# A graph layer on one core: gathers that add to the edge product in place of copy and addition

## The reference

```python
h = concatenate([x[src], edge_attr], axis=1)       # 53125 x (128 + 64)
h = relu(_bn(h @ W1 + b1, g1, be1))                # mean and variance over all edges
s = segment_sum(h, dst); cnt = segment_sum(1, dst)
agg = s / max(cnt, 1)
h2 = relu(_bn(concatenate([x, agg], axis=1) @ W2 + b2, g2, be2))
out = layernorm(x + relu(h2 @ Wl + bl))
```

## Time and profile before

| what | value |
|---|---|
| median of 3 runs | 901.51 us (897.14 to 904.6) |
| profiled execution: span | 892.4 us, 11876 instructions |
| median less that span | 9.1 us |
| POOL / PE / DVE / ACT busy | 461.4 / 455.6 / 389.9 / 235.3 us |
| gathers (L597) | 416, from 52.6 to 725.0 us |
| stretch after them | 167.4 us of the span |

### The profile page before, as it was taken

How to read it: one execution, slowest core, us unless ns; L and a number is a source line. 1 busy time by engine, 2 the same in 40 slices (tenths; PEclk the granted TensorE clock), 3 DMA queues, 4 the chain that set the end, 5 groups by cost and what they waited for, 6 DMA issues and landing times.

```text
span 892.4 us, 11876 instructions
## 1 busy us (share of the span) xinstructions
PE 455.6 (51%) x2195; PEld 345.1 (39%) x2195; DVE 389.9 (44%) x905; ACT 235.3 (26%) x595; POOL 461.4 (52%) x572
## 2 busy tenths in 40 slices
PE   1644454535525455334544543354543349999662
PEld 1622232323323233223332332232332239998542
DVE  1343434334333343333434433244433267776495
ACT  0111122212212122111322222121221135655264
POOL 2046666566665655556666655565655543333352
PEclk9955555555555555555555555555555558999887
DMA  1233322223323222223332322232322224777202
GB/s 64 86 89 88 92 87 80 88 79 94 100 85 88 76 88 88 69 84 94 92 94 76 96 77 77 82 98 72 94 85 71 85 89 131 210 223 226 90 1 72
DMA packets 65229, 83.87 MB, mean 94 GB/s; under 512 B 19159, under 2 KB 44168, under 8 KB 65217
## 3 DMA queue, kind: packets, MB, share of 16 engines
q1 hardware_dynamic: 40529, 39.49, 15.2%
q0 software_dynamic: 13312, 27.29, 11.2%
q10 hardware_dynamic: 11376, 16.97, 5.2%
HBM read 63.61 MB, written 20.08 MB: 94 GB/s over the span
## 4 chain that ended last, share of the span: by engine, by line
another core or an unknown queue 30%; PE 26%; issue 16%; DMA 7%; ACT 6%; DVE 5%; POOL 3%; SPq 2%; ACTq 2%; DVEq 2%; POOLq 1%
PE psH L715 12%; PE psT L709 3%; DMA res<-spill 3%; PE psH L770 3%; PE psC L770 3%; POOL work L597 3%; ACT work L846 2%; ACT res L863 2%; DMA res<-in_x 2%; SPq L404 2%; PE psH L695 1%; PE psC L725 1%; ACTq L857 1%; DMA work<-ytab,idx 1%
## 5 line engine op out<-in xcount | busy, mean ns | idle before, releaser
L597 POOL DMA_INDIRECT work<-ytab,idx x416 | 398.7, 958 | 320.5 <-DVE idx L992 143.3
L715 PE MATMUL psH<-w1e,work 128*128 128x256 f32 x416 | 214.7, 671 | 350.0 <-ACT work L846 254.4
L715 PEld LDWEIGHTS psH<-w1e,work 128*128 128x128 f32 x416 | 121.6, 322 | 409.8 <-ACT work L846 278.1
L1052 DVE TENSOR_TENSOR work<-psH,work 128x512 f32<-128x512 f32 x104 | 71.9, 691 | 235.8 <-remote 104.7
L846 ACT ACTIVATE work<-psT 128x256 f32<-128x256 f32 x104 | 39.9, 384 | 474.2 <-remote 326.2
L1066 DVE TENSOR_TENSOR psX<-work,psX 128x512 f32<-128x512 f32 x104 | 72.1, 693 | 116.7 <-ACT work L861 76.2
L1152 DVE TENSOR_TENSOR work<-res,psX 128x512 f32<-128x512 f32 x103 | 70.7, 688 | 26.5 <-PE psC L770 12.4
L861 ACT ACTIVATE work<-work 128x512 f32<-128x512 f32 x104 | 65.3, 627 | 60.3 <-issue 33.2
L1059 DVE TENSOR_TENSOR psS<-work,psS 128x512 f32<-128x512 f32 x104 | 71.7, 689 | 2.4 <-issue 2.4
L709 PE MATMUL psT<-ident,work 128*128 128x128 f32 x208 | 68.0, 430 | 8.5 <-DMA work<-in_edge_attr 7.7
L617 POOL TENSOR_TENSOR agg<-agg,srci 128x64 f32 x104 | 32.3, 310 | 66.2 <-ACT srci L910 64.5
(11 more groups left out here) (144 smaller groups left out, 336.0 us busy)
## 6 DMA issues: line engine op xcount, KB each, us to landing
work<-in_edge_attr SPq DMA_DIRECT2D x103, 128.0 KB
work<-ytab,idx POOLq DMA_INDIRECT x416
hot_dram<-hotb ACTq DMA_DIRECT2D x26, 256.0 KB
spill<-work ACTq DMA_DIRECT2D x26, 256.0 KB
res<-spill SPq DMA_DIRECT2D x25, 256.0 KB, 2.9
hotb<-hot_dram SPq DMA_DIRECT2D x13, 256.0 KB, 3.9
work<-hot_dram SPq DMA_DIRECT2D x13, 256.0 KB, 3.2
h2x_dram<-agg ACTq DMA_DIRECT2D x25, 125.0 KB
```

Of the source, the lines that this page charges most:

```text
L597: pool.indirect_dma_start(yg[:, q % 2, j * F:(j + 1) * F], None, ytab, bass.IndirectOffsetOnAxis(ap=idx[:, q, j:j + 1], axis=0)).then_inc( ...
L715: last = pe.matmul(psH[q % 2][:, b * 2 * F:(b + 1) * 2 * F], eat[:, q % 2, b * P:(b + 1) * P], w1e[:, :, :].rearrange("p a f -> p (a f)"), ...
L1052: dve.tensor_tensor(hs[:, q % 2, :], psH[q % 2][:, :], yg[:, q % 2, :], ALU.add).then_inc(h_ready, 1)
```

## The change

The rows of the table are no longer gathered into a buffer of their own. ACT first copies the edge product from PSUM to the group's final place, `res` or, for the fourth group of a body, one tile `away` (`part`); then the gather adds the rows of the table to it (`compute_op=ALU.add`). DVE's addition `make_h` and the buffers `yg` and `hs` are gone, as is ACT's copy to `res`; squares and sum read the final place. The gathers take their indices directly from `srci`, so `stage_idx` and `idx` are gone; for this the 104 groups are written out on POOL, without a loop. There are four `gathered` semaphores, one for each group of a body, instead of two.

The order changes as well. PE's step `q` is now the product of `q+2`, the transposes of `q+3`, the counts of `q`. ACT's is the squares of `q`, `part` of `q+2`, `turned` of `q+3`. The hardware loops of PE and ACT have one body less, the last but one being written out too. On POOL a gather waits for `part` of its group and for the sum of the group four back.

```diff
 @block.gpsimd
+            pool.wait_ge(s_idx, 1)
+
             def gather(i, q):
-                if not first(i, q, 2):
-                    pool.wait_ge(h_ready, U * i + q - 1)
-                pool.wait_ge(idx_staged, U * i + q + 1)
-                pool.sem_inc(slot_passed, 1)
+                g = U * i + q
+                if g >= U:
+                    pool.wait_ge(h_summed, g - U + 1)
+                pool.wait_ge(z_ready, g + 1)
+                rows = res[:, (i * KEEP + q) * GF:(i * KEEP + q + 1) * GF] if q < KEEP else away
                 for j in range(TILES):
                     pool.indirect_dma_start(
-                        yg[:, q % 2, j * F:(j + 1) * F], None, ytab,
-                        bass.IndirectOffsetOnAxis(ap=idx[:, q, j:j + 1], axis=0)
-                    ).then_inc(gathered[q % 2], 16)
-
-            for q in range(U):
-                gather(0, q)
-            with pool.Fori(1, NI) as i:
+                        rows[:, j * F:(j + 1) * F], None, ytab,
+                        bass.IndirectOffsetOnAxis(ap=srci[:, j, g:g + 1], axis=0), compute_op=ALU.add
+                    ).then_inc(gathered[q], 16)
+
+            for i in range(NI):
                 for q in range(U):
                     gather(i, q)
 @block.tensor
             def edge_step(i):
+                turned_out = not (isinstance(i, int) and i == NI - 1)
                 for q in range(U):
-                    product(i, q)
-                    if q == 0 and not (isinstance(i, int) and i == 0):
-                        pe.wait_ge(x_out, i)
+                    if q + 2 < U:
+                        product(i, q + 2)
+                    elif turned_out:
+                        product(i + 1, q + 2 - U)
+                    if q + 3 < U:
+                        turn(i, q + 3)
+                    elif turned_out:
+                        turn(i + 1, q + 3 - U)
+                    if q == 2 and turned_out:
+                        pe.wait_ge(x_out, i + 1)
                     counts(i, q)
-                if not (isinstance(i, int) and i == NI - 1):
-                    x_product(i)
+                    if q == 1 and turned_out:
+                        x_product(i)
 @block.scalar
-            def store(i, q):
-                act.wait_ge(h_ready, g + 1)
+            def part(i, q):
+                g = U * i + q
+                act.wait_ge(prod_ready, g + 1)
+                if q == KEEP and not (isinstance(i, int) and i == 0):
+                    act.wait_ge(spilled, 16 * i)
+                    act.wait_ge(sq_ready, g - U + 1)
+                    act.wait_ge(h_summed, g - U + 1)
+                if isinstance(i, int) and i == NI - 1 and q == 0:
+                    act.wait_ge(x_ps, NT)
+                act.sem_inc(slot_passed, 1)
+                act.activation(slot(i, q), psH[q % 2][:, :], ACT.Copy).then_inc(z_ready, 1)
+
+            def squares(i, q):
+                g = U * i + q
+                act.wait_ge(gathered[q], 64 * (i + 1))
...
-                act.activation(sq[:, q % 2, :], hs[:, q % 2, :], ACT.Square).then_inc(sq_ready, 1)
-                if q < KEEP:
-                    act.activation(resg(i, q), hs[:, q % 2, :], ACT.Copy).then_inc(kept, 1)
+                act.sem_inc(slot_passed, 1)
+                act.activation(sq[:, q % 2, :], slot(i, q), ACT.Square).then_inc(sq_ready, 1)
             def edge_step(i):
+                over = isinstance(i, int) and i == NI - 1
                 for q in range(U):
...
+                    squares(i, q)
+                    if q + 2 < U:
+                        part(i, q + 2)
+                    elif not over:
+                        part(i + 1, q + 2 - U)
+                    if q + 3 < U:
+                        turned(i, q + 3)
+                    elif not over:
+                        turned(i + 1, q + 3 - U)
+                    if q == 1 and not (isinstance(i, int) and i == NI - 1):
+                        x_product_out(i)
 @block.vector
             def edge_step(i):
                 for q in range(U):
-                    make_h(i, q)
-                    if not (isinstance(i, int) and i == NI - 1):
-                        stage_idx(i + 1, q)
                     if q < U - 1:
                         onehot_b(i, q + 1)
                     elif not (isinstance(i, int) and i == NI - 1):
                         onehot_b(i + 1, 0)
+                    add_counts(i, q)
                     sum_h(i, q)
-                    add_counts(i, q)
```

More of the change, by code:

```diff
@@ L93, in gnn_kernel @@
         work = sb("work", [P, 6, GF])
-        yg = work[:, 0:2, :]
-        hs = work[:, 2:4, :]
+        away = work[:, 0, :]
         sq = work[:, 4:6, :]
@@ L107, in gnn_kernel @@
         srci = sb("srci", [P, TILES, NG], I32)
-        idx = sb("idx", [P, U, TILES], I32)
         loc = sb("loc", [P, TILES, NG])
@@ L225, in gnn_kernel @@
         prod_ready = sem("ea_product_ready")
-        idx_staged = sem("idx_staged")
-        gathered = [sem(f"gathered{i}") for i in range(2)]
-        h_ready = sem("h_ready")
+        gathered = [sem(f"gathered{i}") for i in range(U)]
+        z_ready = sem("z_ready_in_slot")
         sq_ready = sem("sq_ready")
@@ L232, in gnn_kernel @@
         s_folded = sem("sums_folded")
-        kept = sem("kept")
         spilled = sem("spilled")
@@ L302, in resg, with slot @@
             return res[:, bass.ds((i * KEEP + q) * GF, GF)]
+        def slot(i, q):
+            return resg(i, q) if q < KEEP else away
         def sq_fold(k):
@@ L700, in _, with turn @@
             pe.wait_ge(s_wsgn, 2)
-            def product(i, q):
+            def turn(i, q):
                 g = U * i + q
@@ L710, in product @@
                 last.then_inc(ea_turned, 1)
+            def product(i, q):
+                g = U * i + q
                 pe.wait_ge(eat_ready, g + 1)
                 if not first(i, q, 2):
-                    pe.wait_ge(h_ready, g - 1)
+                    pe.wait_ge(z_ready, g - 1)
                 for b in range(2):
@@ L729, in x_product @@
             def x_product(i):
-                pe.wait_ge(cnt_added, U * i + U - 1)
+                pe.wait_ge(cnt_added, U * i + 1)
                 for h in range(H2):
@@ L737, in edge_step @@
             def edge_step(i):
+                turned_out = not (isinstance(i, int) and i == NI - 1)
                 for q in range(U):
-                    product(i, q)
-                    if q == 0 and not (isinstance(i, int) and i == 0):
-                        pe.wait_ge(x_out, i)
-                    counts(i, q)
-                if not (isinstance(i, int) and i == NI - 1):
-                    x_product(i)
+                    if q + 2 < U:
[8 more added lines that the diff above has]
+                        pe.wait_ge(x_out, i + 1)
+                    counts(i, q)
+                    if q == 1 and turned_out:
+                        x_product(i)
+            turn(0, 0)
+            turn(0, 1)
+            product(0, 0)
+            turn(0, 2)
+            product(0, 1)
             edge_step(0)
-            with pe.Fori(1, NI - 1) as i:
+            with pe.Fori(1, NI - 2) as i:
                 edge_step(i)
+            edge_step(NI - 2)
             edge_step(NI - 1)
@@ L846, in turned @@
                 act.activation(eat[:, q % 2, :], psT[q % 2][:, 0:2 * P], ACT.Copy).then_inc(eat_ready, 1)
-            def store(i, q):
+            def part(i, q):
                 g = U * i + q
-                act.wait_ge(h_ready, g + 1)
+                act.wait_ge(prod_ready, g + 1)
[10 more added lines that the diff above has]
+                act.wait_ge(gathered[q], 64 * (i + 1))
                 if q == KEEP:
-                    act.dma_start(spill[bass.ds(i, 1), :, :].rearrange("a p f -> (a p) f"), hs[:, q % 2, :]
-                                  ).then_inc(spilled, 16)
+                    act.dma_start(spill[bass.ds(i, 1), :, :].rearrange("a p f -> (a p) f"), away).then_inc(spilled, 16)
                 elif q == KEEP - 1:
@@ L874, in edge_step @@
             def edge_step(i):
+                over = isinstance(i, int) and i == NI - 1
                 for q in range(U):
[L876 to L880, removed]
-                if not (isinstance(i, int) and i == NI - 1):
-                    x_product_out(i)
+                    squares(i, q)
[9 more added lines that the diff above has]
+                        x_product_out(i)
             act.wait_ge(s_idx, 1)
             turned(0, 0)
+            turned(0, 1)
+            part(0, 0)
+            turned(0, 2)
+            part(0, 1)
             edge_step(0)
             act.wait_ge(s_tab, TAB)
-            with act.Fori(1, NI - 1) as i:
+            with act.Fori(1, NI - 2) as i:
                 edge_step(i)
+            edge_step(NI - 2)
             edge_step(NI - 1)
@@ L1010, in _ @@
             link(dve.tensor_copy(srci[:, :, :].rearrange("p j g -> p (j g)"), psS[:, 0:TILES * NG]))
-            for q in range(U):
```

(8 more changed lines are left out.)

2 lines of the change are left out of this document (removed).

## The result

The changed kernel takes 997.82 us (median of 4 runs, 996.13 to 998.16) against 901.45 us of the kernel before beside it (4 runs, 897.14 to 904.6): slower, ratio 1.1074, 95% interval 1.1025 to 1.1122. Where the executions of a kernel fall into a quicker and a slower group, ratios and intervals here compare the quicker ones alone. The profiled execution has a span of 996.4 us; 892.4 before.

What follows compares the result with a forecast made beforehand. It took POOL's gather pitch, 1.26 us, as the floor: last gather at 580.5 instead of 724.97, with the end -145.2, giving 756, plus 37 for PE's late answers: 793 us, range 748 to 938.

Steps and rivals of the forecast that it cites:

- the lower end: POOL's gathers: adding in flight costs nothing, so a gather stays at 0.958 us.
- The upper end: POOL's gathers: three row ends instead of two make a gather 1.44 us, +0.48.
- The second rival: POOL's 416 gathers become dear: with +0.48 us each, pitch 1.74, 956 us in all; chance 0.26.
- 157.6 us of waits: POOL's waits before gathers, 143.3 us for staged indices and 14.3 for DVE's addition: what a better edge loop can return.
- PE's late answers: PE's results come late while POOL issues gathers: ten pieces of 13.5 to 13.8 us, taken as a property that may stay.
- The 37 us: Edge loop: the part of PE's late answers not covered by working two groups ahead, added to 756 us.
- the first rival: Edge loop, clean POOL bound: the new order dissolves PE's late answers, so the 37 us go too, 756 us; chance 0.20.
- ten of them last 13.7, so 3.6 stick out of each: Edge loop: two groups ahead cover 10.1 us of each late answer of PE, leaving 36 us.
- The third rival: Before gathers, POOL waits for the product instead of the index, same 157.6 us: about 904 us; chance 0.08.

Runs made afterwards that it cites:

- e1_plain: The changed kernel with gathers that overwrite instead of adding: 754.65 us, beside 753.75 for the kernel before; ratio 1.001.
- e2_add_alone: The kernel before with only its gathers made to add into their buffer: 990.82 us, where the kernel before takes 753.75.
- The half gathers: The changed kernel with gathers over 64 partitions instead of 128, adding and plain: 944.36 and 864.47 us, one run each on a slow chip.
- e7_before_here: The kernel before, unchanged, profiled again on another occasion: 890.92 us.
- e5_in_place: The kernel before, order and DVE additions kept, with indices in place and gathers written out: 750.97 us beside 753.75; ratio 0.9973.
- e9_plain_again: The changed kernel with overwriting instead of adding gathers, run again on a slow chip: 885.73 us beside 900.68 for the kernel before.
- e10_in_place_again: The kernel before with indices in place and gathers written out, run again on a slow chip: 888.26 us beside 900.68.

## Why the prediction was wrong

**The bound.** Right: POOL's pitch is the floor, and the changed kernel runs on it with 3.6 us of waits between its first and last gather.

**The step that failed: "I take the lower end, the nearest row being the same instruction with the same operands".** The price of adding in flight was taken as 0 us a gather. It is 0.60 (e1_plain, e2_add_alone and the profile after agree), 250 us over 416 gathers. The upper end was too low as well: +0.48 came from taking the whole instruction for writing descriptions of rows. The half gathers show that rows are a small part of it, by the estimate above 0.7 ns each in a plain gather; most of a gather is a fixed 0.87 us, and most of the price is a fixed 0.42. So a price in proportion to the rows' ends had no ground, and what the fixed part is spent on stays open. The second rival is what happened, place and sum: with the measured pitch its formula gives 56.3 + 416 x 1.855 = 828 us for the last gather, and it ended at 831.3. It had a chance of 0.26; the range ended at 938 us, since it held gathers up to 1.39 us alone.

**Where the price shows, and the index copies.** By "DMA: Bandwidth & Descriptors" (SWDGE vs HWDGE vs iDMA) of the Trainium skill, the descriptors of such a DMA are made by a program on GpSimd. The trace of e2_add_alone agrees in where the price appears: POOL is busy for 1.552 us a gather. That the time goes into descriptors no run shows. By "SBUF — State Buffer" (SBUF: two separate sides) of the Trainium skill, a DVE copy in a two-port mode keeps GpSimd from writing descriptors, so gathers could gain from the removal of the index copies. They took 955 ns at the median with copies (e7_before_here) and without (e5_in_place), so nothing came back, as forecast; whether these small copies ran in such a mode no run shows.

**The idleness.** The forecast was that 157.6 us of waits would go and 37 come back, for PE's late answers. In fact the waits fell to 3.6 us, issue rose by 6.5, and no late answer was left, because the pitch was 1.86. The 37 us were mis-sized for the case that the forecast had in mind, too. On a quick chip there are none: e1_plain takes 755 us, the 756 of the first rival. On a slow one e9_plain_again waits 119 us and takes 886, not 793. So even with adding at no price the forecast would have been 93 us too low there. The step behind it is "ten of them last 13.7, so 3.6 stick out of each": it counted only the ten longest pieces, where ACT alone waits 326.2 us for late transposes, in 38 waits, and it let two groups ahead hide 10.1 us of each. The third rival, the wait that only changes its name, was wrong for the changed kernel. In e10_in_place_again, in the old order, its pattern shows: the 143 us moved from the index to the addition. In e9_plain_again, in the new order, POOL waits mostly for the sum and not, as that rival has it, for the product.

**Small terms.** DVE's busy time fell by 58 us, not by the 93 of its additions and copies: the groups fell by 91, but neighbouring instructions overlap. The first gather came at 57.46 (56.3 forecast). The landing after the last gather took 833.14 - 831.28 = 1.9 us (1.8 before), so adding didn't delay it. ACT's copy from PSUM took 0.58 to 0.60 us (0.60). The DMA engines' share of the gathers doubled, from 11.2 to 22.9%, hidden. The stretch after the gathers lasted 165.1 us (165 forecast). The sum by the prediction's own steps, with 1.855 for 1.26 and no late answers: 828 instead of 724.97, less 0.7, is +102; measured +104 in span.

**How much it loses depends on the base.** The changed kernel takes 997 to 998 us in both sets of runs. Against a kernel before of 897 to 901 that is 11 to 13%. Where that one takes 754 it would be 32%; this pair was not run on one chip, but e2_add_alone with 991 against 754 was. Taking `compute_op` out of the changed kernel gains 243 us where that leads to 755 (e1_plain), and 112 where it leads to 886 (e9_plain_again): on a slow chip the late answers that come back eat up the rest.

## What to carry to other kernels

Here, fusing an operation into a transfer moved its cost to the engine that issues the transfer. Price it there first: 72 us of DVE additions, of which POOL waited for 14.3, became 250 us on the engine that sets the pace. Before blaming a wait on the instruction named in the profile, run the kernel with that instruction gone; here the wait moved next door at the same length. And time the kernel before beside every run: here it took 754 or 900 us depending on the chip.

## What the runs showed of the hardware

- **An indirect gather is paid mostly by the instruction.** POOL is busy for 0.955 us with 128 rows of 512 bytes, for 0.911 us with 64. Adding in flight: 1.552 and 1.418 us. All gathers together are 59904 packets with adding and 13312 without; the first number fits one packet a row (416 x 128) and 16 completions a gather (416 x 16), which is an estimate.
- **The same kernel took 753 to 754 us in three sets of runs, on three chips, and 897 to 901 in three others**, a difference of 19%. Where one kernel was traced on both kinds (e5_in_place and e10_in_place_again), every gather is equal and so is the clock. The loss is idle time in which, as far as the traces tell, PE's results reach ACT and DVE late: in the earlier trace rows ACT starts 13.7 us after PE has taken up the transposes. It appears with plain gathers every 1.26 us, in every order tried (old, new, further ahead), and with half the rows every 1.21 us; not with a start every 1.72, 1.77 or 1.86 us. Pitches between 1.26 and 1.72 were run on quick chips only. What differs between the chips, and why PE is late, the runs don't show.
- A lead of four groups for POOL, worth 0.7% on a quick chip, came out at 988 us against 901 on a slow one. That the longer lead is what hurts was argued, not shown.
